# Block 1's scan in chunks of 64 tokens, with the feed-forward down product and the gate product inside it

## The chip, the cores and the metric

The kernel runs on one NeuronCore of one Trainium2 chip. The metric is the device time of one execution in microseconds; the median of the runs shown is taken. TensorE is PE here (PEld its weight loads), VectorE DVE, ScalarE ACT, GpSimd POOL, and SyncE SP, which only issues DMAs.

## The reference, cut to what matters

Block 0 (a top-k attention and a mixture of 64 experts) takes most of the time and is hardly touched. Block 1, on 2 x 512 tokens of 256 channels, is

```
xn = layernorm(x)
r, k, v = mixes of xn and the previous token, times Wr, Wk, Wv    # 32 heads of 8
g = silu(mix @ Wg.T)
w = exp(-exp(time_decay)); u = time_faaaa
step(state, (rc, kc, vc)):                      # one chunk of Q tokens, per head
    att = rc @ kc * w_mat                       # w^(i-j-1) for i > j, u for i == j, else 0
    yc  = att @ vc + rc @ state * w^i
    state = w^Q * state + (kc * w^(Q-1-j)) @ vc
y  = group-normalised over each head of 8 channels, * gamma + beta
x  = x + (y * g) @ Wo.T + relu(xn @ Wfc.T)^2 @ Wproj.T             # ternary Wfc, Wproj
```

The chunk length Q doesn't change the values, apart from rounding.

## The kernel before, in words

Each engine has its own program, and semaphores tie them together; nothing is reordered by a planner. After the last expert, SP loads the routed sums back (racc), then the five weights of block 1 (w5), the decay, bonus and mix rows (s_l1c) and gamma and beta. DVE adds the sums, takes statistics and applies the layer norm (L880), POOL raises the variance to -0.5 (rsqrt, L529), PE transposes and runs the feed-forward up products, and ACT writes relu (L793) and, between them, the decay masks wmask, one exp of 128 columns for each of the 32 heads (L795). DVE squares the relu (L1155) and mixes (mixture, L1170).

Then PE runs, each for all eight token tiles of 128: k and r transposed (project_T), the feed-forward down product, transposes of k (L1548), the v product and the g product (L1312 is the helper product's line for all of these). DVE adds the down product to xs (L1198), scales k (kn, L1211), and adds the bonus to the diagonal of each head's mask (L1216); ACT copies v and takes tanh of g, and DVE multiplies (L1221). All banks are shared in turn.

The scan has 16 units u: token tile t = u // 2 and half of the heads f = u % 2. PE writes a unit's scores for 16 heads as four matmuls, one for each group of 32 rows (L1576); DVE multiplies each bank of 512 columns by the mask (L1290); PE adds the state's part (L1586) and the masked scores times v in 32-column tiles (L1592), and the next state's product (L1604), which DVE masks and adds to the decayed state (state_update, L1227, L1228). PE turns y back (y_natural, L1612). The group norm of earlier tiles is spread between the masks: means and variances on DVE (L1243 to L1256), centring on POOL (centred, L608), the square on ACT (L822), the root on ACT (group_std, L818) with a reciprocal and a Newton step on DVE (group_scale, L1263 to L1273), and four products and sums on POOL (gated, L618 to L624). At the end PE transposes z and multiplies by Wo, DVE adds (L1306), and SP stores each tile.

At the very start POOL issues two DMAs that fill the routed tables with zeros (L522), and then runs block 0's two rsqrt (L529).

## Time and profile before

| | us |
|---|---|
| median of 3 runs (603.67 to 606.5) | 604.94 |
| profiled execution, its own time | 603.5 |
| profiled execution, span of the instructions | 601.8 |
| mean granted share of TensorE's clock | 0.892 |

Over the span PE is busy for 457.6 us (76%), DVE for 340.9 (57%), POOL for 344.0 (57%) and ACT for 194.5 (32%). Times of rows are microseconds from the start of the span. A row of a group gives its count (x), what ended the idle time before it (<-), and its mean in ns where it says so. Ends of matmuls are modelled, so the starts are read.

### The profile page before, as it was taken

To read this page: it belongs to the slowest core of one execution; us is meant where nothing else is said; L and a number is where in the kernel's file an instruction comes from. 1 tells how busy PE (TensorE), PEld (TensorE's weight loads), DVE (VectorE), ACT (ScalarE), POOL (GpSimd) and SP (SyncE) were. 2 spreads that over 40 slices of the span, in tenths; PEclk is the share of its full clock that TensorE was granted. 3 is DMA by queue.
4 is the path that set the end of the run, shared out by engine and by line. 5 is a ranking of instruction groups with operands and counts; after the bars stand their busy time and mean duration, and the time that the engine had idled before them with its cause. 6 is when DMAs were issued, how large, how long until landed. Compare 5 with 4: busy or idle time off the path is not lost.

```text
span 601.8 us, 8652 instructions
## 1 busy us (share of the span) xinstructions
PE 457.6 (76%) x2288; PEld 281.7 (47%) x2288; DVE 340.9 (57%) x931; ACT 194.5 (32%) x512; POOL 344.0 (57%) x327
## 2 busy tenths in 40 slices
PE   2840870688878887677678777989489989999977
PEld 1620430255545554444445444658334678455546
DVE  4799995144434444354343543542567548696983
ACT  1423220233424344343343343431074604021112
POOL 6057777777777777777787777752024001033443
PEclk9985795697879989999998997989789999797997
DMA  8511618266878778888787887863500000000002
GB/s 305 213 26 32 169 23 209 58 159 164 210 181 228 193 189 201 206 185 203 179 216 189 193 199 178 223 129 88 186 0 2 0 0 1 1 2 1 2 2 70
DMA packets 49984, 75.40 MB, mean 125 GB/s; under 512 B 14553, under 2 KB 31289, under 8 KB 49785
## 3 DMA queue, kind: packets, MB, share of 16 engines
q1 hardware_dynamic: 32968, 53.74, 30.1%
q0 software_dynamic: 16992, 21.38, 19.2%
q8 instruction: 11, 0.18, 0.1%
q14 instruction: 13, 0.10, 0.1%
HBM read 58.31 MB, written 15.99 MB: 123 GB/s over the span
## 4 chain that ended last, share of the span: by engine, by line
POOL 42%; PE 23%; issue 20%; DVE 8%; DMA 3%; ACT 3%; SPq 0%; POOLq 0%; DVEq 0%; ACTq 0%
POOL big L544 20%; PE ps L1312 14%; POOL routed L558 11%; POOL big L551 10%; PE ps L1576 4%; DVE big L1290 2%; DMA routed<-big 2%; PE ps L1592 2%; DMA big<-in_maa 1%; PE ps L1317 1%; ACT big L795 1%; DVE big L915 1%; DVE big L912 1%; DVE big L919 1%; PE ps L1586 1%
## 5 line engine op out<-in xcount | busy, mean ns | idle before, releaser
L1312 PE MATMUL ps<-big 128*128 128x352 f32 (+4 forms) x768 | 227.8, 445 | 17.7 <-ACT big L719 14.8
L1312 PEld LDWEIGHTS ps<-big 128*128 128x128 f32 (+2 forms) x768 | 147.6, 202 | 78.0 <-ACT big L719 25.4
L544 POOL DMA_INDIRECT big<-val_tab,big x128 | 125.4, 980 | 62.4 <-issue 38.7
L558 POOL DMA_INDIRECT routed<-big x64 | 104.3, 1630 | 34.1 <-issue 17.1
L1020 DVE SCALAR_TENSOR_TENSOR big<-big,ps 128x176 f32<-128x176 f32 x64 | 21.6, 337 | 104.3 <-ACT big L714 104.3
L1317 PE MATMUL ps<-cst,big 128*128 128x128 f32 x144 | 31.4, 307 | 57.7 <-DMA big<-tok_tab,big 55.6
L551 POOL DMA_INDIRECT big<-tok_tab,big x64 | 61.5, 962 | 22.6 <-issue 17.7
L1028 DVE COPY big<-ps 88x256 f32<-88x256 f32 x64 | 26.9, 420 | 67.9 <-PE ps L1404 67.3
L709 ACT ACTIVATE big<-ps 128x256 f32<-128x256 f32 x64 | 24.6, 384 | 110.5 <-PE ps L1317 108.9
L1317 PEld LDWEIGHTS ps<-cst,big 128*128 128x128 f32 x144 | 17.6, 150 | 76.9 <-DMA big<-tok_tab,big 51.9
L1312 PE MATMUL ps<-xnT,big 128*128 128x512 f32 (+1 forms) x104 | 51.4, 652 | 2.1 <-ACT xnT L646 2.1
L719 ACT ACTIVATE big<-ps,big 128x256 f32<-128x256 f32 x64 | 30.2, 472 | 57.6 <-DMA routed<-big 48.9
L1290 DVE TENSOR_TENSOR big<-ps,big 128x512 f32<-128x512 f32 x64 | 42.0, 678 | 2.5 <-PE ps L1576 2.2
L1576 PE MATMUL ps<-big 32*128 32x512 f32 x128 | 36.3, 697 | 3.0 <-DVE big L1290 2.0
L725 ACT ACTIVATE big<-ps 128x512 f32<-128x512 f32 x64 | 34.5, 595 | 0.9 <-PE ps L1421 0.8
L714 ACT ACTIVATE big<-ps 128x176 f32<-128x176 f32 x64 | 20.4, 318 | 43.8 <-PE ps L1312 43.4
L1312 PEld LDWEIGHTS ps<-xnT,big 128*128 128x128 f32 (+1 forms) x104 | 20.8, 206 | 28.5 <-issue 26.9
L1404 PE MATMUL ps<-cst,big 128*88 128x128 f32 x128 | 27.0, 295 | 0.0
L1317 PE MATMUL ps<-cst,xn 128*128 128x128 f32 x48 | 10.5, 344 | 20.9 <-DVE xn L880 17.9
L608 POOL TENSOR_TENSOR xn<-xn,gst 128x256 f32<-128x256 f32 x8 | 5.0, 629 | 35.6 <-DVE gst L1246 35.6
L1404 PEld LDWEIGHTS ps<-cst,big 128*88 128x88 f32 x128 | 15.1, 130 | 20.7 <-issue 16.3
L597 POOL MEMSET big<- 128x2560 f32 x1 | 2.2, 2237 | 39.2 <-ACT big L809 39.2
(179 smaller groups left out, 617.2 us busy)
## 6 DMA issues: line engine op xcount, KB each, us to landing
big<-in_w SPq DMA_DIRECT2D x64, 352.0 KB
big<-in_w SPq DMA_DIRECT2D x64, 160.0 KB
big<-q_dram SPq DMA_DIRECT2D x144, 32.0 KB
routed<-big POOLq DMA_DIRECT2D x2, 1152.0 KB, 12.3
big<-val_tab,big POOLq DMA_INDIRECT x128, 2.3
big<-routed SPq DMA_DIRECT2D x4, 512.0 KB, 4.6
q_dram<-big SPq DMA_DIRECT2D x24, 64.0 KB
tok_tab<-xn SPq DMA_DIRECT2D x1, 1280.0 KB, 5.5
```

Of the source, the lines that this page charges most:

```text
L544: nc.gpsimd.indirect_dma_start(vals[:, group, side, c, :], None, val_tab, bass.IndirectOffsetOnAxis(ap=vidxT[:, col:col + 1], axis=0))\
L551: nc.gpsimd.indirect_dma_start(xe[:, e % SLOTS, :], None, tok_tab, bass.IndirectOffsetOnAxis(ap=sidx[:, e:e + 1], axis=0))\
L558: nc.gpsimd.indirect_dma_start(routed[e % 2], bass.IndirectOffsetOnAxis(ap=sidx[:, e:e + 1], axis=0), ye[:, e % 2, :], None, compute_op=AL ...
L709: nc.scalar.activation(xeT[:, u % 2, :, :], PS[0][:, 0:D].rearrange("p (c n) -> p c n", c=DC), ACT.Copy).then_inc(s_xeT, 1)
L719: nc.scalar.activation(ye[:, u % 2, :], PS[3][:, 0:D], ACT.Copy, scale=gate).then_inc(s_y, 1)
L725: nc.scalar.activation(ex[:, c, :], PS[4 + c % 2][:, :], ACT.Exp).then_inc(s_ex, 1)
L1028: nc.vector.tensor_copy(heT[:, u % 2, :, :], PS[2][0:IC, 0:2 * P].rearrange("p (c n) -> p c n", c=2))\
L1290: nc.vector.tensor_tensor(aring[:, a % 8, :].rearrange("p (h n) -> p h n", h=4), PS[q][:, :].rearrange("p (h n) -> p h n", h=4), wmask[:, ...
L1312: last = nc.tensor.matmul(o, w, m, start=(n == 0), stop=(n == len(pairs) - 1))
L1317: last = nc.tensor.transpose(bank[:, c * P:(c + 1) * P], src[:, c * P:(c + 1) * P], ident)
L1404: last = nc.tensor.transpose(PS[2][0:IC, c * P:(c + 1) * P], hm[:, u % 2, c * IC:(c + 1) * IC], ident)
L1576: nc.tensor.matmul(PS[q][:, :], kT[rows, f, tok(t)], rhead[rows, f, :, tok(t)], start=True, stop=True).then_inc(s_a1p, 1)
```

## The change

- A chunk is 64 tokens. The two chunks of a token tile lie on partitions 0 to 63 and 64 to 127: scores go as 32 x 64 tiles of 256 columns, outputs as 64 x 32 tiles of 64 columns into two banks, and one mask product covers two banks (masked), so there are two for a unit. wmask is 32 heads of 64 columns.
- The state is kept in a ring of four. PE multiplies the old one by a diagonal matrix of the chunk's decay (wdiag) and adds the new product in the same bank; DVE masks and copies it (state_copy). There are 14 such steps, seven for each batch.
- The feed-forward down product and the g product of each tile are issued in the scan, into PS[7], which y_natural uses as well. ACT copies the down product out (ff_copy), and POOL adds it to xs (x2_add).
- The squares and the causal mask go to POOL, the bonus goes onto the diagonal in eight operations of 512 columns, mixture(3) writes xnT.
- The group norm's root is one pow on POOL (group_rsqrt).
- SP issues the small rows of block 1 ahead of the routed sums; POOL runs block 0's rsqrt ahead of the zero fills.

The core of the diff, with the indent cut; removed functions are shown above:

```diff
 "vrow": H0 * np.array([[S - 1, 0, S + S - 1, S]]) + p,
 "slot": p,
-"jdec": P - 1 - p,
+"jdec": Q1 - 1 - p % Q1,
...
 oT_at = [(), (0, 1, 2), (3, 4, 5), (6, 7)]
 SLOTS = 4
 UNITS = B * TPB * 2
+STATE_AT = []
+for u in range(UNITS):
+    b, n = u // 8, u % 8 + 1
+    STATE_AT.append(7 * b + n if n < NQ - 1 else 7 if u == 7 else None)
...
     for u in range(SLOTS):
         next_weights(E // SLOTS - 1, u, slice(E // SLOTS - 1, E // SLOTS))
     sp.wait_ge(s_lp, NG * 4)
+    sp.wait_ge(s_y, E + 1)
+    sp.dma_start(edrow, td_row.partition_broadcast(P)).then_inc(s_l1c, 16)
+    sp.dma_start(urow, u_row.partition_broadcast(P)).then_inc(s_l1c, 16)
+    sp.dma_start(edcol, td_col).then_inc(s_l1c, 16)
+    sp.dma_start(maat, maa).then_inc(s_l1c, 16)
     for i in range(2):
         sp.wait_ge(s_sc[i], 16 * (1 + E // 2))
         for b in range(B):
             sp.dma_start(racc[i][:, b * TPB:(b + 1) * TPB, :],
                          routed[i][b * S:(b + 1) * S, :].rearrange("(t p) d -> p t d", p=P))\
               .then_inc(s_racc[i][b], 16)
-    sp.wait_ge(s_y, E + 1)
     sp.dma_start(w5, w_rkvgo).then_inc(s_w5, 16)
-    sp.dma_start(edrow, td_row.partition_broadcast(P)).then_inc(s_l1c, 16)
...
     sp.dma_start(gb[:, 0, :], gamma.partition_broadcast(P)).then_inc(s_gb, 16)
     sp.dma_start(gb[:, 1, :], beta.partition_broadcast(P)).then_inc(s_gb, 16)
...
     last.then_inc(s_fill, 1)
     pool.wait_ge(s_fill, 5)
+    def rsqrt(n, half):
+        t = slice(half * TPB, (half + 1) * TPB)
+        pool.wait_ge(s_var, B * n + half + 1)
+        nc.gpsimd.tensor_tensor(rstd[:, 1, t], rstd[:, 0, t], rsm[:, 2, t], ALU.pow).then_inc(s_rstd, 1)
+    for half in range(B):
+        rsqrt(0, half)
     for i in range(2):
         nc.gpsimd.dma_start(routed[i].rearrange("(r p) d -> p r d", p=P),
                             zero[:, 0:D].rearrange("p (a d) -> p a d", a=1).broadcast_to([P, PAD // P, D]))\
           .then_inc(s_sc[i], 16)
...
     last.then_inc(s_wh, 1)
-    pool.wait_ge(s_wm1, 1)
...
+    def square(i):
+        pool.wait_ge(s_relu, i + 1)
+        h = hf[:, i % FC, (i // FC) * S:(i // FC + 1) * S]
+        nc.gpsimd.tensor_tensor(h, h, h, ALU.mult).then_inc(s_sq, 1)
+    def causal(i):
+        w = wmask[:, i * HH:(i + 1) * HH, :]
+        pool.wait_ge(s_wm1[i], 1)
+        nc.gpsimd.tensor_tensor(w, w, const("causal").unsqueeze(1).broadcast_to([P, HH, Q1]), ALU.mult)\
+          .then_inc(s_wmc, 1)
+    for i in range(4):
+        square(i)
+    causal(0)
+    square(4)
+    causal(1)
+    for i in range(FC, 2 * FC):
+        square(i)
+    nc.gpsimd.memset(gst[:, 2, 0:H1], -0.5)
+    nc.gpsimd.memset(vpr[0], 0.0).then_inc(s_vd, 1)
     pool.wait_ge(s_mix, 4)
+    nc.gpsimd.memset(vpr[1], 0.0).then_inc(s_vd, 1)
     pool.wait_ge(s_v1, NT)
-    nc.gpsimd.memset(vpr, 0.0).then_inc(s_vd, 1)
-    pool.wait_ge(s_vd, 1)
+    pool.wait_ge(s_vd, 2)
     def heads_and(t, k):
...
+    def group_rsqrt(t):
+        pool.wait_ge(s_gv, t + 1)
+        g = [gst[:, k, (t % 4) * H1:(t % 4 + 1) * H1] for k in range(2)]
+        nc.gpsimd.tensor_tensor(g[1], g[0], gst[:, 2, 0:H1], ALU.pow).then_inc(s_gr, 1)
     def gated(t):
         z = xn[:, t, 0:D]
         y, g = heads_and(t, 1)
+        group_rsqrt(t)
         if t == 0:
             pool.wait_ge(s_gbh, 1)
...
+        pool.wait_ge(s_g, t + 1)
         pool.wait_ge(s_gr, t + 1)
         nc.gpsimd.tensor_tensor(y, y, g, ALU.mult).then_inc(s_zs, 1)
...
+            x2_add(t - 1)
         if t >= 2:
             centred(t - 2)
         if t >= 3:
             gated(t - 3)
+    x2_add(NT - 1)
     centred(NT - 2)
     gated(NT - 3)
...
+    def ff_copy(t):
+        act.wait_ge(s_ffd, t + 1)
+        if t >= 2:
+            act.wait_ge(s_x2, t - 1)
+        nc.scalar.activation(ffo[:, t % 2, :], PS[7][:, 0:D], ACT.Copy).then_inc(s_ffo, 1)
+    def gate_tanh(t):
         act.wait_ge(s_gp, t + 1)
...
+        nc.scalar.activation(gn[:, t, :], PS[7][:, 0:D], ACT.Tanh, scale=0.5).then_inc(s_gt, 1)
...
+    def y_copy(t):
+        act.wait_ge(s_ynp, t + 1)
+        nc.scalar.activation(xn[:, t, 0:D], PS[7][:, 0:D], ACT.Copy).then_inc(s_yn, 1)
     for t in range(NT):
         for f in range(2):
             u = 2 * t + f
-            act.wait_ge(s_yTp, u + 1)
...
+            (ff_copy, gate_tanh)[f](t)
+            act.wait_ge(s_yTp, 2 * u + 2)
+            nc.scalar.activation(yTs[:, u % 4, :, :], ps[:, 4:6, 0:Q1], ACT.Copy).then_inc(s_yT, 1)
             if t >= 1:
-                (group_squares, group_std)[f](t - 1)
...
+                (y_copy, group_squares)[f](t - 1)
+    y_copy(NT - 1)
     group_squares(NT - 1)
     for t in range(NT):
-        if t == 2:
-            group_std(NT - 1)
         act.wait_ge(s_zTp, t + 1)
...
     ln_apply(1, 1)
-    def square(i):
...
+    def diagonal(i):
+        dve.wait_ge(s_wmc, i // 2 + 1)
+        h = slice(8 * i, 8 * i + 8)
+        link(nc.vector.tensor_tensor(udiag, const("diag").unsqueeze(1).broadcast_to([P, 8, Q1]),
+                                     urow[:, h].unsqueeze(2).broadcast_to([P, 8, Q1]), ALU.mult))
+        link(nc.vector.tensor_tensor(wmask[:, h, :], wmask[:, h, :], udiag, ALU.add))
     for i in range(4):
         f, n = divmod(i, 2)
         dve.wait_ge(s_kTp, i + 1)
         nc.vector.tensor_copy(kT[:, f, n * S:(n + 1) * S], PS[i][:, :]).then_inc(s_kf, 1)
-    mixture(2)
     for i in range(4):
...
         dve.wait_ge(s_rTp, i + 1)
-        nc.vector.tensor_tensor(rw[:, f, cols].rearrange("p (t n) -> p t n", n=P),
...
+        nc.vector.tensor_tensor(rw[:, f, cols].rearrange("p (t n) -> p t n", n=Q1),
+                                PS[4 + i][:, :].rearrange("p (t n) -> p t n", n=Q1),
+                                wb[:, f, :].unsqueeze(1).broadcast_to([P, NQ, Q1]), ALU.mult).then_inc(s_rw, 1)
...
-    mixture(3)
...
                                 kdec.unsqueeze(2).broadcast_to([P, H1, HN]), ALU.mult).then_inc(s_kn, 1)
-    dve.wait_ge(s_wmc, 1)
...
+    for i in range(4):
+        diagonal(i)
+    dve.wait_ge(s_wall, 1)
+    for f in range(2):
+        note(nc.vector.tensor_scalar(wdiag[:, f, :], ident, wall[:, f:f + 1], None, ALU.mult))
     settle()
-    for t in range(NT):
+    mixture(3)
+    def gate(t):
         dve.wait_ge(s_gt, t + 1)
-        nc.vector.scalar_tensor_tensor(gn[:, t, :], gn[:, t, :], 1.0, PS[t % 4][:, 0:D], ALU.add, ALU.mult)\
+        nc.vector.scalar_tensor_tensor(gn[:, t, :], gn[:, t, :], 1.0, PS[7][:, 0:D], ALU.add, ALU.mult)\
           .then_inc(s_g, 1)
-    def state_update(u):
...
+    def state_copy(k):
+        b, n = divmod(k, NQ - 1)
+        dve.wait_ge(s_kvp, k + 1)
+        nc.vector.tensor_tensor(state[:, (NQ * b + n + 1) % 4, :, :],
+                                PS[6][:, 0:2 * P].rearrange("p (f n) -> p f n", f=2),
+                                const("heads").unsqueeze(1).broadcast_to([P, 2, P]), ALU.mult)\
+          .then_inc(s_st, 1)
     def norm_parts(t):
...
+    norm_stages = (group_means, group_variances)
+    def masked(u, k):
+        a = 2 * u + k
+        dve.wait_ge(s_a1p, 4 * a + 4)
+        if a >= 8:
+            dve.wait_ge(s_yTp, 2 * (a // 2 - 3))
+        h = HH * (u % 2) + 8 * k
+        nc.vector.tensor_tensor(aring[:, a % 8, :].rearrange("p (q n) -> p q n", q=2),
+                                ps[:, 2 * k:2 * k + 2, 0:4 * Q1],
+                                wmask[:, h:h + 8, :].rearrange("p (q h) n -> p q (h n)", q=2),
+                                ALU.mult).then_inc(s_a1, 1)
+    state_copy(0)
     for u in range(UNITS):
-        if u % 8 == 0:
...
         for q in range(4):
-            a = 4 * u + q
...
+            if q % 2 == 0:
+                masked(u, q // 2)
+            elif q == 1:
+                if STATE_AT[u - 1:u] and STATE_AT[u - 1] is not None:
+                    state_copy(STATE_AT[u - 1])
+                if u >= 2 and u % 2 == 0:
+                    gate(u // 2 - 1)
             for stage, norm in enumerate(norm_stages):
                 t, odd = divmod(u - 3 - stage, 2)
                 if t >= 0 and not odd:
                     norm(t, q)
-        if u >= 1 and (u - 1) % 8 < 6:
...
+    gate(NT - 1)
+    for norm, t in ((group_variances, NT - 2), (group_means, NT - 1), (group_variances, NT - 1)):
         for step in range(4):
             norm(t, step)
     for t in range(NT):
         dve.wait_ge(s_op, t + 1)
+        dve.wait_ge(s_x2, t + 1)
         nc.vector.tensor_tensor(xs[:, t, :], PS[4 + t % 4][:, 0:D], xs[:, t, :], ALU.add).then_inc(s_o, 1)
...
-        product(PS[t % 4][:, 0:D], [(hf[:, c, tok(t)], w_pj1[:, c, :]) for c in range(FC)]).then_inc(s_ffd, 1)
...
         if t >= 4:
             pe.wait_ge(s_kn, t - 3)
         for f in range(2):
-            last = nc.tensor.transpose(PS[4 + t % 4][:, f * P:(f + 1) * P], kT[:, f, tok(t)], ident)
+            last = nc.tensor.transpose(PS[t % 4][:, f * P:(f + 1) * P], kT[:, f, tok(t)], ident)
         last.then_inc(s_knp, 1)
...
...
+        product(PS[t % 4][:, 0:D], [(mixed(2, c, tok(t)), w5[:, 2, c, :]) for c in range(DC)])\
+            .then_inc(s_v1p, 1)
+    def ff_down(t):
+        pe.wait_ge(s_sq, FC * (1 + t // TPB))
+        if t >= 1:
...
+            pe.wait_ge(s_g, t)
+        product(PS[7][:, 0:D], [(hf[:, c, tok(t)], w_pj1[:, c, :]) for c in range(FC)]).then_inc(s_ffd, 1)
+    def gate_product(t):
+        pe.wait_ge(s_mix, 4)
+        pe.wait_ge(s_yn, t) if t else pe.wait_ge(s_ffo, 1)
+        product(PS[7][:, 0:D], [(mixed(3, c, tok(t)), w5[:, 3, c, :]) for c in range(DC)]).then_inc(s_gp, 1)
+    def chunk(t, c):
+        return slice(t * P + c * Q1, t * P + (c + 1) * Q1)
+    def scores(u, k):
         t, f = divmod(u, 2)
-        for q in range(4):
...
+        if u:
+            pe.wait_ge(s_a1, 2 * (u - 1) + k + 1)
+        for q in (2 * k, 2 * k + 1):
             rows = slice(RG * q, RG * (q + 1))
-            nc.tensor.matmul(PS[q][:, :], kT[rows, f, tok(t)], rhead[rows, f, :, tok(t)],
-                             start=True, stop=True).then_inc(s_a1p, 1)
+            for c in range(2):
+                nc.tensor.matmul(PS[q][c * Q1:(c + 1) * Q1, 0:4 * Q1], kT[rows, f, chunk(t, c)],
+                                 rhead[rows, f, :, chunk(t, c)], start=True, stop=True).then_inc(s_a1p, 1)
     def outputs(u):
         t, f = divmod(u, 2)
         b, g = divmod(t, TPB)
-        y = PS[4 + u % 2]
...
+        if u >= 1:
+            pe.wait_ge(s_yT, u)
+        for c in range(2):
+            n = 2 * g + c
+            if n:
+                pe.wait_ge(s_st, 7 * b + n)
+                nc.tensor.matmul(PS[4 + c][:, 0:Q1], state[:, (NQ * b + n) % 4, f, :], rw[:, f, chunk(t, c)],
+                                 start=True, stop=False, skip_group_check=True)
+        pe.wait_ge(s_a1, 2 * u + 2)
+        pe.wait_ge(s_vd, t + 3)
         for h in range(4):
-            for q in range(4):
...
+            for c in range(2):
+                rows = slice(c * Q1, (c + 1) * Q1)
+                for q in range(4):
+                    at = (q % 2 * 4 + h) * Q1
+                    last = nc.tensor.matmul(PS[4 + c][32 * q:32 * q + 32, 0:Q1],
+                                            vpr[t % 2][rows, 4 * f + q, 32 * h:32 * h + 32],
+                                            aring[rows, (2 * u + q // 2) % 8, at:at + Q1],
+                                            start=(h == 0 and 2 * g + c == 0), stop=(h == 3),
+                                            skip_group_check=True)
+                if h == 3:
+                    last.then_inc(s_yTp, 1)
+    def state_product(k):
+        b, n = divmod(k, NQ - 1)
+        t, c = divmod(NQ * b + n, 2)
+        rows = slice(c * Q1, (c + 1) * Q1)
+        if k:
+            pe.wait_ge(s_st, k)
+        if n:
+            for f in range(2):
+                nc.tensor.matmul(PS[6][:, f * P:(f + 1) * P], wdiag[:, f, :], state[:, (NQ * b + n) % 4, f, :],
+                                 start=(f == 0), stop=False, skip_group_check=True)
+        for f in range(2):
+            last = nc.tensor.matmul(PS[6][:, f * P:(f + 1) * P], kn[rows, t, f * P:(f + 1) * P],
+                                    vn[rows, t, f * P:(f + 1) * P], start=(n == 0 and f == 0), stop=True,
+                                    skip_group_check=True)
+        last.then_inc(s_kvp, 1)
     def y_natural(t):
         pe.wait_ge(s_yT, 2 * t + 2)
-        if t >= 1:
-            pe.wait_ge(s_yn, t)
+        if t < NT - 1:
+            pe.wait_ge(s_ffo, t + 2)
+        else:
+            pe.wait_ge(s_g, NT)
         for f in range(2):
-            last = nc.tensor.transpose(PS[7][:, f * P:(f + 1) * P], yTs[:, f, 0:P], ident)
+            last = nc.tensor.transpose(PS[7][:, f * P:(f + 1) * P],
+                                       yTs[:, (2 * t + f) % 4, :, :].rearrange("p c n -> p (c n)"), ident)
         last.then_inc(s_ynp, 1)
-    pe.wait_ge(s_g, NT)
     pe.wait_ge(s_v1, NT)
-    scores(0)
+    pe.wait_ge(s_rh, 4)
+    scores(0, 0)
+    scores(0, 1)
+    state_product(0)
     for u in range(UNITS):
         if u + 1 < UNITS:
-            scores(u + 1)
+            scores(u + 1, 0)
+        (ff_down, gate_product)[u % 2](u // 2)
+        if u + 1 < UNITS:
+            scores(u + 1, 1)
+        outputs(u)
+        if STATE_AT[u] is not None:
+            state_product(STATE_AT[u])
         if u >= 2 and u % 2 == 0:
             y_natural(u // 2 - 1)
-        outputs(u)
-        state_product(u)
     y_natural(NT - 1)
     def z_transposes(t):
         pe.wait_ge(s_z, t + 1)
         if t == 0:
-            pe.wait_ge(s_a1, 4 * UNITS)
+            pe.wait_ge(s_a1, 2 * UNITS)
         if t >= 2:
             pe.wait_ge(s_zT, t - 1)
         transposes(xn[:, t, 0:D], PS[t % 2], s_zTp)
```

## Rows read from the trace of the kernel before

**Rows 1.** the page, its first line.

```profile
span 601.8 us, 8652 instructions
```

**Rows 2.** busy time by stage, busy us (x) of each engine.

```profile
...
474.90:492.20 17.30, 17.30 (x83) 15.18 (x82) 4.02 (x10) 6.21 (x11) 0.00 (x0) 1.00 0.00 0
511.70:582.70 71.00, 67.58 (x710) 37.41 (x710) 59.60 (x147) 12.22 (x36) 20.99 (x34) 0.90 0.01 2
582.70:601.80 19.10, 12.19 (x50) 9.67 (x50) 8.90 (x24) 4.30 (x14) 8.59 (x13) 0.82 0.16 55
```

**Rows 3.** the chain of waits by line, 566 to 575 us.

```profile
...
by line: DVE big L1290 48.6%; issue 20.8%; DVE gst L1253 9.0%; DVE gst L1256 7.8%; DVE big L1227 4.7%; DVE gst L1243 3.7%; DVE gst L1263 2.9%; DVE gst L1266 1.2%; DVE gst L1273 1.1%; DVE gst L1246 1.0%; DVE big L1228 0.7%; DVEq L1288 0.7%; 
```

**Rows 4.** groups by line on DVE in the scan.

```profile
...
L1290 DVE TENSOR_TENSOR big<-ps,big 128x512 f32<-128x512 f32 x64 | 42.0, 678 | 2.5 <-PE ps L1576 2.2 <-issue 0.2
```

**Rows 5.** PE in one unit; x4: to 522.99, x12: to 523.2.

```profile
...
522.44 0.49 PE L1586 MATMUL ps<-big 128*128 128x128 f32 x2
...
522.86 0.32 PE L1592 MATMUL ps<-big 128*32 128x128 f32 x4
...
522.86 0.54 PE L1592 MATMUL ps<-big 128*32 128x128 f32 x12
...
522.86 1.08 PE L1592 MATMUL ps<-big 128*32 128x128 f32 x32
523.87 0.49 PE L1604 MATMUL ps<-big 128*128 128x128 f32 x2
```

**Rows 6.** the chain of waits before the scan: start, us, what.

```profile
...
496.88 13.99 PE ps L1312 x64
...
513.01 0.70 DVE big L1290
```

**Rows 7.** DVE in order of time before the scan: start, us, line.

```profile
...
474.92 0.69 DVE L1193 TENSOR_TENSOR big<-ps,wb 128x512 f32<-128x512 f32 x1 [1.02 <-PE ps L1312]
...
492.52 2.47 DVE L1170 SCALAR_TENSOR_TENSOR big<-big,xnT 128x1024 f32<-128x1024 f32 x2
494.91 2.74 DVE L1211 TENSOR_TENSOR big<-ps,big 128x256 f32<-128x256 f32 x8
```

**Rows 8.** DVE and POOL side by side in the scan.

```profile
...
566.86 0.73 POOL L622 TENSOR_TENSOR xn<-xn,gb 128x256 f32<-128x256 f32 x1
566.92 0.70 DVE L1256 TENSOR_SCALAR gst<-gst 128x32 f32<-128x32 f32 x1
```

**Rows 9.** after the last expert, in order of time.

```profile
...
414.33 9.78 SPq L491 DMA_DIRECT2D big<-routed  x4
...
418.57 0.47 ACT L719 ACTIVATE big<-ps,big 128x256 f32<-128x256 f32 x1 [7.83 <-PE ps L1312]
...
430.75 1.05 POOL L529 TENSOR_TENSOR rstd<-rstd,rsm 128x4 f32<-128x4 f32 x1 [9.87 <-DVE rstd L875]
433.76 0.23 ACT L779 ACTIVATE big<-big 128x32 f32<-128x32 f32 x1 [14.72 <-DMA big<-in_maa]
...
434.67 1.37 DVE L880 TENSOR_SCALAR xn<-xs,mv,rstd 128x256 f32<-128x256 f32 x4
```

**Rows 10.** the start of the kernel, in order of time.

```profile
...
5.84 2.34 POOL L522 DMA_DIRECT2D routed<-big  x2 [0.32 <-POOL big L517]
...
8.32 2.18 POOL L529 TENSOR_TENSOR rstd<-rstd,rsm 128x4 f32<-128x4 f32 x2
```

**Rows 11.** busy time of PE during the 64-column products.

```profile
...
28.25:31.60 3.35, 3.35 (x32) 1.00 0.45 160
```

**Rows 12.** groups of weight loads, two stretches.

```profile
...
L1312 PEld LDWEIGHTS ps<-big,xnT 128*128 128x128 f32 x55 | 8.1, 191 | 0.6
...
L1592 PEld LDWEIGHTS ps<-big 128*32 128x32 f32 x512 | 14.2, 117 | 3.6 <-DVE big L1290 1.4 <-issue 0.5
```

**Rows 13.** ACT's last square, in order of time.

```profile
...
587.11 0.42 ACT L822 ACTIVATE big<-xn 128x256 f32<-128x256 f32 x1 [2.81 <-POOL xn L608]
```

**Rows 14.** groups on POOL: busy us, mean ns.

```profile
...
L529 POOL TENSOR_TENSOR rstd<-rstd,rsm 128x4 f32<-128x4 f32 x4 | 4.2, 1060 | 17.5 <-DVE rstd L875 17.4
```

More of the change, by code:

```diff
@@ L57 @@
 CONST = {}
-for _name, _n in (("ident", P), ("pdist", P), ("steps", P), ("heads", P), ("tokinv", NT), ("vrow", 4), ("slot", 1),
+for _name, _n in (("ident", P), ("pdist", 64), ("steps", 64), ("diag", 64), ("causal", 64), ("heads", P), ("tokinv", NT), ("vrow", 4), ("slot", 1),
                   ("jdec", 1), ("hrow", NV4)):
@@ L336, in block_kernel @@
         s_kdec = sem("key_decay_exp")
-        s_wm1 = sem("decay_tables_exp")
+        s_wall = sem("chunk_decay_exp")
+        s_wm1 = [sem(f"decay_tables_exp{i}") for i in range(2)]
         s_wmc = sem("decay_mask_causal")
```

183 lines of the change are left out of this document (42 added, 141 removed).

## The prediction

> **What bounds the kernel now.** I read the span first [rows 1], then busy time by stage [rows 2], because the change touches only the part after the experts (from 424 us on) and one line at the start. Four stages follow each other there: the feed-forward down products (474.9 to 492.2), a short step of transposes, the v and g products (to 511.7), the scan (to 582.7) and a tail. In the first PE is busy throughout at full clock: it is worth what PE takes. The third is so too, as the next part shows. The scan is different. Its chain of waits is nearly half mask multiplications on DVE, L1290, and the rest is small DVE work [rows 3]; these multiplications, 64 of 0.68 us, idle only 2.5 us ahead of them [rows 4]. PE also reads 67.6 of 71 us there, but most of that is scores that stand behind a mask still to be freed. So the scan is DVE's, at 71 / 16 = 4.4 us a unit (a token tile and half of the heads), and PE's own need must be added up.
>
> **What PE needs per unit.** One unit's PE rows [rows 5]: the 32 output instructions (each matmul is two passes) start in fours (from 522.86 on, four by 522.99 and twelve by 523.20): one four each 0.11. Eight fours are 0.87 us, and the next product starts 1.01 us after the first: a block of small tiles costs 0.14 over its passes. A state product, two passes of 0.107 on the full array between tiled blocks, takes 0.42: a full block costs 0.2 over its passes, its first weight load being uncovered. PE now needs scores 0.99 + state 0.42 + outputs 1.01 + state product 0.42 + 0.14 = 3.0 us of 4.4.
>
> **The change, ahead of the scan.** The down products leave (17.3 us [rows 2]) and the eight g products (32 instructions at 13.99 / 64 = 0.219 us, 7.0 us [rows 6]); they come back below. What then ends this stretch is DVE. It finishes r's multiplication at 475.6 [rows 7], then mixture(2) 2.5 (478.1), gamma and beta 0.4, eight kn 2.7 (481.3). diagonal() issues eight 128x512 operations, each followed by its own wait: priced like L1290 with 0.07 for the wait, 6.0 (487.3). wdiag 0.4, mixture(3) 2.5 (490.2), first state copy and first mask 1.2: 491.4. PE has the v products at 487.3 and the first scores at 488.3, and waits. Today the first mask ends at 513.7 [rows 6]. That is 22.3 us less, whatever stands in the loop. The squares and the causal mask go to POOL: ten 128x512 products at some 1.3 us and two of 1024 columns at 2.5 us, scaled from 0.73 us for 256 [rows 8], 18 us between 442 and 466; they are needed in the loop only (s_sq) and by diagonal (480), so they cost nothing; uncovered, the last of them could be 14 us later before anything waits.
>
> **Two moved queues.** SP issues the four block 1 rows ahead of the loads of routed. Today the last of them lands at 433.7, and behind it stand ACT's exp and then, on DVE, three small operations ahead of ln_apply(1,0), which starts at 434.67 though rstd was there at 431.8 [rows 9]. The gain is at most 2.9. But routed's first two loads, now issued at 414.3, come behind the last expert's scaled output (419.0) and four issues of 0.5 us, at about 421; with 4.6 us to land, DVE's three routed additions start 2.5 us late, and end about 1 us late, since the last waited for its own load before. I take 1.6; bounds 0 and 2.9. At the start POOL's two rsqrt pass the zero fills (5.84 to 8.2 [rows 10]): DVE can go on at 8.4 instead of 9.4, when it has done the second half's statistics: 1.0, handed on through the top-k, bounds 0 and 1.9. Together 2.6.
>
> **The loop after.** Per unit, at full clock:
> - scores: twice four matmuls of 256 columns, two passes of 0.216, + 0.14: 1.14
> - down product (even units) 17.3 / 8 = 2.16 + 0.2; g product (odd) 0.87 + 0.2
> - state part of the outputs: four instructions of 64 columns on full weights. The nearest row says that these don't get shorter with the columns: 3.35 us for about 31 of them, 0.11 each [rows 11]: 0.45 + 0.2 = 0.65
> - outputs: 64 instructions of 64 columns in 32-column tiles on half the rows. If eight run side by side, eight groups of 0.054 to 0.11; a 32-column load takes 0.12 against 0.19 for 128 columns [rows 12], so it isn't what held the row above at 0.11. I take 0.06: 0.48 + 0.14 = 0.62. Upper bound: the halves take turns, 16 groups at 0.11, 1.9
> - state product: four passes on the decay's full weights, four on half the rows, each 0.43 + 0.2: 1.26
> - y_natural (even) 0.27.
>
> A pair is 6.30 + 4.74 = 11.04, eight pairs 88.3; the last unit has no scores (1.14), three loop units no state product and one no decay (4.4), four units only one state read (0.9), and unit 0 no y_natural (0.3): 81.6. Waits: an even unit's down product stands behind gate() on DVE, which is queued behind state_copy: 0.3 to leave PE, 0.35, 0.42, hand-overs 0.06, against 0.77 for the switch and scores: 0.35 x 7 = 2.4. Some 0.1 at each of 14 state steps: 1.4. The granted clock was 0.90 over the scan's 71 us [rows 2]: with levels of 1.2 and 2.4 GHz that is 14 us at the low one, or 7 lost, around PE's waits at its start and for the second batch's first mask. The new loop has one such start, and full products in it: I take 2.5; bounds 0 and 10. Sum 87.9, against 69.0 from the first mask today. DVE needs two masks 1.36, state copy 0.45, half a gate 0.2 and half the means and variances 0.6: 2.6 us a unit of 5.5, so it is no bound.
>
> The scan ends 22.3 + 2.6 - 18.9 = 6.0 us earlier.
>
> **The tail and pow.** Today ACT's last square ends at 587.53 [rows 13] and the kernel 14.3 us later, 19.1 after the last outputs. group_scale's ACT and DVE steps become one pow on POOL, on 32 columns. The trace has pow on 4: 1.06 us [rows 14], where an addition of 256 takes 0.73 [rows 8]. Lower bound 1.06 (all fixed), upper 8 x 0.95 + 0.1 = 7.7 (all by column). The nearest row is pow's own, so I take 2.0, twice that. A gated() is then 3.15 + p long. After the last outputs (T) POOL has centred(6), gated(5), centred(7) at T + 2.6 + p, gated(6), gated(7): z of the last tile at T + 9.55 + 3p, end at T + 13.9 + 3p; the other way, over the last square, it ends at T + 18 + p. With p = 2: T + 20.0 by either, 0.9 more than today. In the loop POOL needs 5 + p a tile of 11: covered up to p = 5.5.
>
> **A rule against the change.** A DVE tensor_scalar on 32 columns took 0.70 and ended with POOL's addition beside it [rows 8]. The Trainium skill (SBUF — State Buffer, Who interferes with whom) says that the pair is an exclusive lock held for a whole instruction, taken by fast DVE modes and by DVE operations with two SBUF inputs; this trace agrees for the first. By it, mixtures would stand behind squares on POOL; at 451 to 457 POOL waits for exps anyway, and the masks read PSUM, so it adds nothing to the sum except that means and variances can wait for a pow, with 5 us of slack a pair.
>
> **Sum.** 601.8 - 6.0 + 0.9 = 596.7 us span; the profiled execution took 603.5, 1.7 over its span, and the median is 1.4 above that: 599.8 us.
>
> **Rivals.**
> - pow by column (0.18). For: 4 columns of pow already cost more than 256 of an addition. Against: the fixed part may be most of it. From p = 3.7 the end at T + 13.9 + 3p has eaten the whole gain; at 7.7 it is T + 37, 17 more than forecast, and POOL bounds the loop too: 616 to 620. This decides the other side: slower. The Trainium skill (GPSIMD Engine Reference, Performance pitfalls for Q7 kernels) says that a dependent fp32 chain pays about 4 cycles for each element, which speaks for this case; no row here shows pow on more than 4 columns.
> - The output tiles don't run eight at a time (0.10). For: no row has tiles on half the rows. 1.9 instead of 0.62 adds 20: 620; two turns of short groups (16 x 0.06) add 0.48 x 16 = 7.7: 607.
> - The clock stays low in more of the loop, as small tiles follow each other, or PE's waits for ACT and DVE around the one bank PS[7] are longer than 0.35 (0.14): 5 to 8 us more, 605 to 608.
> - The forecast, 0.58: 590 to 606.
>
> The low end has pow at 1.1 (-0.9), no lost clock and no waits (-6.3), outputs at 0.054 (-0.8) and more from the moved queues (-1.8): 590. The high end reaches into the first two rivals, 614.
>
> Within 0.5% (3.0 us) is what a measurement of this kernel can't tell from no change: 601.9 to 608.0. Faster is most of the forecast's case, 0.53; same its upper end, two turns of tiles and the third rival, 0.19; slower pow and turns of full length, 0.28.
>
> **What would show it.** Loop pairs near 11 us, the down product 0.35 behind a gate; output starts in eights; DVE under two thirds busy in the scan, against 84% now; pow's mean near 2; the first mask's end near 489, the last outputs near 577; ACT's last exp no longer waiting for block 1's rows. I am wrong first if pow is long or the outputs come in fours.

## The result, and the profile after

The changed kernel took 613.12 us (median of 4 runs, 611.8 to 614.01), the kernel before 605.72 beside it: a ratio of 1.0113, 95% interval 1.0057 to 1.0169. A second comparison gave 1.018 (1.0145 to 1.0216). It is slower by 7 to 11 us; 599.8 was forecast, with slower at 0.28. Ratios below are to the kernel before on the same chip. That kernel's own runs spread over 597 to 610 us, and the first outputs of the scan began anywhere from 492 to 498 us in versions of the changed kernel that are the same up to there. So the experiments are also read by two stretches inside one execution: from the start of the first outputs to the start of the last (83.6 us in the changed kernel, in each of four profiles: twice as it is, e2 and e5), and from the end of the last outputs, T, to the end of the span. I call the second one the tail.

The span of the profiled execution (own time 611.8 us) stands against [rows 1]; the two windows, columns as in [rows 2], hold the loop and the tail.

```profile
span 610.0 us, 10034 instructions
...
487.90:577.50 89.60, 86.29 (x1523) 60.08 (x1526) 33.52 (x78) 14.84 (x44) 54.70 (x50) 0.98 0.01 2
577.50:610.00 32.50, 14.25 (x88) 10.45 (x80) 5.31 (x15) 4.24 (x12) 24.58 (x16) 0.68 0.10 33
```

The scan is now PE's (96% busy, DVE 37%), and the last outputs start at 577.08 and last 0.86 (the line below): T = 577.9, 4.7 us earlier than the 582.7 before. The tail is 32.1 us against 19.1, 13.0 more. 13.0 - 4.7 = 8.3, and the spans differ by 8.2. So the whole loss is in the tail, and there POOL is busy for 24.6 of 32.5 us.

```profile
577.08 0.86 PE L1625 MATMUL ps<-big 64*32 64x64 f32 x64
```

The two tails repeat from profile to profile: 19.0 to 19.1 us in three profiles where the tail is as before, 32.1 in both of the changed kernel. T doesn't: where nothing but the tail or idle POOL time was touched in the kernel before, it was at 577.2 (e1) and 577.5 (e10) as well. So the 4.7 us of this pair of profiles are no measure of what the change gains up to T; the ratios give one at the end of the experiments.

POOL's groups, from the scan to the end (busy us, mean ns, idle before):

```profile
L647 POOL TENSOR_TENSOR gst<-gst 128x32 f32<-128x32 f32 x8 | 43.5, 5442 | 0.0
L660 POOL TENSOR_TENSOR xn<-xn,gb 128x256 f32<-128x256 f32 x8 | 5.8, 727 | 0.6
```

L647 is pow on 32 columns: 5.44 us, against 1.06 on 4 columns in [rows 14] and the 2.0 that the forecast took. A product of 256 columns takes 0.73. The chain of waits in the tail shows three of them one behind the other, for tiles 5, 6 and 7 (start, us, what):

```profile
576.26 0.63 POOL xn L642
576.89 5.41 POOL gst L647
...
582.43 0.64 POOL xn L658
...
585.47 0.59 POOL xn L642
586.05 5.41 POOL gst L647
...
594.64 5.41 POOL gst L647
...
603.27 0.69 PE ps L1350 x2
603.96 3.43 PE ps L1345 x8
```

Inside the scan, the same view over a pair of units. The reader is to see that every piece but one short stretch is PE's: scores (L1604), state part (L1616), outputs (L1625), state product (L1642 the decay, L1645 the new part), y_natural (L1657), with down (x10) and g (x4) under L1345.

```profile
546.08 0.42 DVE big L1264
...
546.63 2.40 PE ps L1345 x10
549.03 0.59 PE ps L1604 x8
549.62 0.59 PE ps L1616 x4
550.21 0.79 PE ps L1625 x53
551.00 0.64 PE ps L1642 x4
551.64 0.64 PE ps L1645 x4
552.28 0.37 PE ps L1657 x2
...
553.24 1.08 PE ps L1345 x4
...
558.50 1.53 PE ps L1345 x6
```

From one down product to the next is 558.50 - 546.63 = 11.87 us. What PE still waits for in the scan, in us, times and longest, is DVE's gate, L1264:

```profile
PE ps L1345 <- DVE big L1264: 2.7, 7, 0.7
```

After the last expert, ACT's exp follows the four small loads and the layer norm starts 3.2 us earlier than the 434.67 of [rows 9]:

```profile
416.82 1.55 POOL L574 DMA_INDIRECT routed<-big  x1 [7.30 <-ACT big L766]
...
422.58 0.23 ACT L826 ACTIVATE big<-big 128x32 f32<-128x32 f32 x1 [6.04 <-DMA big<-in_maa]
423.93 1.23 DVE L1173 TENSOR_TENSOR xs<-xs,big 128x1024 f32<-128x1024 f32 x1 [3.12 <-DMA big<-routed]
...
431.45 1.38 DVE L929 TENSOR_SCALAR xn<-xs,mv,rstd 128x256 f32<-128x256 f32 x4
```

But POOL's scatter of the last expert (the first line) is 2.5 us earlier too. Before, it was

```profile
419.32 1.55 POOL L558 DMA_INDIRECT routed<-big  x1 [7.30 <-ACT big L719]
```

From the scatter to the layer norm it is 14.6 us, and 15.35 before (14.95 in e1 and in e10, which have the order of before).

### The profile page after: what moved, and what is told of

It reads as the page before. It is cut to its first block, busy times and chain, and to the rows that moved or that the text cites. A ratio compares the mean times of both kernels' runs of the same rounds, so it can differ in the third digit from the quotient of the medians.

```text
span 610.0 us, 10034 instructions
## 1 busy us (share of the span) xinstructions
PE 463.8 (76%) x3032; PEld 288.9 (47%) x3032; DVE 300.0 (49%) x807; ACT 193.0 (32%) x511; POOL 400.8 (66%) x356
## 3 DMA queue, kind: packets, MB, share of 16 engines
q0 software_dynamic: 16992, 21.38, 19.1%
## 4 chain that ended last, share of the span: by engine, by line
POOL 41%; PE 25%; issue 20%; DMA 6%; DVE 6%; ACT 2%; POOLq 0%; ACTq 0%; DVEq 0%
POOL big L560 19%; PE ps L1345 15%; POOL big L567 9%; POOL routed L574 9%; DMA routed<-big 4%; POOL gst L647 3%; PE ps L1604 2%; PE ps L1625 2%; PE ps L1645 1%; PE ps L1616 1%; PE ps L1642 1%; PE ps L1350 1%; DVE big L964 1%; DVE big L961 1%; DMA big<-routed 1%
## 5 line engine op out<-in xcount | busy, mean ns | idle before, releaser
L1345 PE MATMUL ps<-big 128*128 128x352 f32 (+3 forms) x736 | 227.0, 454 | 18.5 <-ACT big L766 13.6
L1345 PEld LDWEIGHTS ps<-big 128*128 128x128 f32 (+1 forms) x736 | 143.5, 206 | 82.3 <-issue 27.0
L756 ACT ACTIVATE big<-ps 128x256 f32<-128x256 f32 x64 | 24.6, 385 | 97.8 <-PE ps L1350 97.3
L1345 PE MATMUL ps<-xnT,big 128*128 128x512 f32 (+1 forms) x104 | 52.2, 660 | 2.1 <-ACT xnT L693 2.1
L647 POOL TENSOR_TENSOR gst<-gst 128x32 f32<-128x32 f32 x8 | 43.5, 5442 | 0.0
L1345 PE MATMUL ps<-big,xnT 128*128 128x256 f32 (+1 forms) x128 | 32.3, 401 | 8.2 <-ACT xnT L889 7.6
L1345 PEld LDWEIGHTS ps<-xnT,big 128*128 128x128 f32 (+1 forms) x104 | 20.9, 207 | 28.6 <-issue 27.0
L1345 PEld LDWEIGHTS ps<-big,xnT 128*128 128x128 f32 x128 | 23.9, 216 | 15.1 <-ACT xnT L889 7.9
L1437 PEld LDWEIGHTS ps<-cst,big 128*88 128x88 f32 x128 | 15.4, 132 | 22.3 <-issue 18.0
L1312 DVE TENSOR_TENSOR big<-ps,big 128x512 f32<-128x512 f32 x32 | 21.1, 683 | 4.2 <-PE ps L1604 4.2
```

The costliest lines, as they stand in the source:

```text
L647: nc.gpsimd.tensor_tensor(g[1], g[0], gst[:, 2, 0:H1], ALU.pow).then_inc(s_gr, 1)
L756: nc.scalar.activation(xeT[:, u % 2, :, :], PS[0][:, 0:D].rearrange("p (c n) -> p c n", c=DC), ACT.Copy).then_inc(s_xeT, 1)
L1345: last = nc.tensor.matmul(o, w, m, start=(n == 0), stop=(n == len(pairs) - 1))
L1437: last = nc.tensor.transpose(PS[2][0:IC, c * P:(c + 1) * P], hm[:, u % 2, c * IC:(c + 1) * IC], ident)
```

## The experiments

The leading theory (A) is that pow on 32 columns, three times in POOL's queue behind the last outputs, is the loss. Its rivals: pow is only slow beside other work (B in the first), the tail is long for other reasons (B in the second), the scan itself is the loss (C).

**What pow costs by its size.** The kernel before, with seven unused pows on POOL before the scan:

```diff
+nc.gpsimd.memset(gst[:, 0, 0:64], 0.7)
+nc.gpsimd.memset(gst[:, 1, 0:64], -0.5).then_inc(s_probe, 1)
+for i, n in enumerate((1, 2, 4, 8, 16, 32, 64)):
+    pool.wait_ge(s_probe, i + 1)
+    nc.gpsimd.tensor_tensor(gst[:, 2, 0:n], gst[:, 0, 0:n], gst[:, 1, 0:n], ALU.pow).then_inc(s_probe, 1)
```

> The kernel before, with seven pow instructions of 1, 2, 4, 8, 16, 32 and 64 columns added on POOL while it idles before the scan; the result is not used. Theory A (pow is paid by the column): a line through the two sizes seen so far, 1.07 us at 4 columns and 5.44 at 32, gives 0.6, 0.8, 1.1, 1.7, 2.9, 5.4 and 10.4 us. Theory B (pow itself is short, about 2 us at 32 columns as forecast, and the 5.44 us come from the work beside it in the scan, on the shared SBUF or on a late operand): alone it takes near 2 us at 32 columns and under 3 at 64.

Groups by shape on POOL in that kernel:

```profile
L600 POOL TENSOR_TENSOR gst<-gst 128x64 f32<-128x64 f32 x1 | 10.5, 10547 | 0.1
...
L600 POOL TENSOR_TENSOR gst<-gst 128x32 f32<-128x32 f32 x1 | 5.4, 5426 | 0.1
L600 POOL TENSOR_TENSOR gst<-gst 128x16 f32<-128x16 f32 x1 | 2.9, 2903 | 0.1
...
L600 POOL TENSOR_TENSOR gst<-gst 128x8 f32<-128x8 f32 x1 | 1.6, 1635 | 0.1
...
L600 POOL TENSOR_TENSOR gst<-gst 128x4 f32<-128x4 f32 x1 | 1.0, 1006 | 0.1
...
L600 POOL TENSOR_TENSOR gst<-gst 128x1 f32<-128x1 f32 x1 | 0.6, 570 | 0.1
```

Theory A, on its numbers. From 32 columns to 64 it is 5.12 us more, 0.160 a column; from 16 to 32 it is 0.158; what is left over is 0.3 to 0.4. The 5.43 us come ahead of the scan, where DVE has only a few operations beside it, and with one fixed value (0.7); in the scan it is 5.44. So neither the scan's work nor the values have a part in them.

**Pow on 4 columns in the changed kernel**, and **pow twice**:

```diff
-nc.gpsimd.tensor_tensor(g[1], g[0], gst[:, 2, 0:H1], ALU.pow).then_inc(s_gr, 1)
+nc.gpsimd.tensor_tensor(g[1][:, 0:4], g[0][:, 0:4], gst[:, 2, 0:4], ALU.pow).then_inc(s_gr, 1)
```

> The changed kernel with pow on 4 of the 32 columns, so the other 28 heads are not normalised rightly; all else is issued as before. Theory A (three pows of 5.44 us stand in POOL's queue behind the last outputs): by the forecast's own formula the end comes at T + 18 + p with p = 1.1, 19.1 us behind the last outputs instead of 32.1: 13 us less than the changed kernel, so about 600 us or 0.99 of the kernel before. Theory B (the tail is long for the rest of POOL's queue, its added additions to xs, and for PE at its low clock): at most the last pow leaves the path, 4.4 us less, 608 to 609 us. Theory C (the scan itself is the loss): no change worth the name, 611 to 613.

Measured: 0.993 (0.9897 to 0.9963), 599.35 us, on a chip where the kernel before took 602.95. Scan 83.6 us, unchanged; tail 579.4 to 596.6, 17.3 us instead of 32.1. That is 14.8 us off the tail for 13 expected, and this kernel, in which 28 of the 32 heads miss their root, is faster than the one before: theories B and C fall. The tail beats the 19.1 that was worked out by 1.8. From the last square's end (583.49) it is 13.1 us, where the kernel before took 14.3 with the clock granted at 0.82 in its tail; here it was 0.90:

```profile
579.35:596.60 17.25, 11.05 (x50) 8.85 (x50) 5.59 (x14) 4.22 (x12) 10.95 (x15) 0.90 0.19 62
```

```diff
 nc.gpsimd.tensor_tensor(g[1], g[0], gst[:, 2, 0:H1], ALU.pow).then_inc(s_gr, 1)
+pool.wait_ge(s_gr, 2 * t + 1)
+nc.gpsimd.tensor_tensor(g[1], g[0], gst[:, 2, 0:H1], ALU.pow).then_inc(s_gr, 1)
...
-pool.wait_ge(s_gr, t + 1)
+pool.wait_ge(s_gr, 2 * t + 2)
```

> The changed kernel with each tile's pow issued twice, the same result written twice. Theory A: three more pows of 5.44 us and a wait each behind the last outputs, 16.5 us, and POOL's need for a tile rises to about 12.3 us against 11.9 for a pair of units, which adds up to 3 us more by the end of the scan: 629 to 634 us. Theories B and C: 5.5 us more at most, 618 or less.

Measured: 1.0773 (1.0728 to 1.0819), 650.28 us. The direction is A's, the size a miss. The tail is 53.3 us, 21.2 more; the scan is 100.9 us from first to last outputs, 17.3 more, where up to 3 were expected. My need of POOL for a tile was wrong: from the groups of the changed kernel it is 5.44 + 0.63 (centring) + 2.81 (the four products) + 0.73 (x2_add) + 0.40 (copy of v) = 10.0, with some 0.5 of hand-overs 10.5, not 6.8. A second pow makes it 15.9; centrings follow each other at 567.61 and 583.47, 15.86 apart, and PE waits (clock 0.86 in the loop's window, from 0.98). So with one pow POOL is covered in the scan by only 1.4 us a pair (11.87 - 10.5).

**The two queue moves alone**, in the kernel before:

```diff
+for half in range(B):
+    rsqrt(0, half)
 for i in range(2):
     nc.gpsimd.dma_start(routed[i]...)
-for half in range(B):
-    rsqrt(0, half)
...
 sp.wait_ge(s_lp, NG * 4)
+sp.wait_ge(s_y, E + 1)
+sp.dma_start(edrow, ...)   # and urow, edcol, maat
 for i in range(2):
     sp.wait_ge(s_sc[i], 16 * (1 + E // 2))
```

> The kernel before with the two queue moves alone (the four small loads of block 1 ahead of the loads of the routed sums, and POOL's two early root operations ahead of the zero fills). The forecast's term: 2.6 us less, so 603.1; from the changed kernel's trace, where the layer norm of block 1 starts 3.2 us earlier, 3.2 less. Rival: what comes first is given back where PE waits for the value projections and the feed-forward products anyway, 0 to 0.5 us.

Measured: 0.9962 (0.9923 to 1.0001), 600.67 us: 2.3 us less, near the forecast's 2.6, though the interval just reaches no change. The rival's 0 to 0.5 isn't excluded by it. The traces show the two moves apart. Behind the top-k PE starts at 61.9, 61.9 and 62.9 us in the three profiles with POOL's old order, and at 60.4 to 62.1 in the eleven with the new one, 1.2 earlier on average, for 1.0 forecast. From the last scatter to the layer norm it is 15.35, 14.95 and 14.95 with SP's old order and 14.5 to 14.9 with the new one, 0.4 less on average, where 1.6 was taken.

**The roots of the last three tiles off POOL.** Tiles 0 to 4 keep pow; behind the last tanh ACT takes three roots, and DVE does the reciprocal and the Newton step (group_scale as before):

```diff
-group_rsqrt(t)
+if t < NT - 3:
+    group_rsqrt(t)
...
 y_copy(NT - 1)
+group_std(NT - 3)
+group_std(NT - 2)
 group_squares(NT - 1)
+group_std(NT - 1)
```

> The changed kernel with the roots of the last three tiles as in the kernel before (ACT takes the root, DVE the reciprocal and a Newton step), behind the last tanh; tiles 0 to 4 keep pow. Theory A (three pows of 5.44 us on POOL behind the last outputs are the loss): POOL has only the products left, three tiles of 3.15 us and a centring, the last of them done about 13 us behind the last outputs, the end about 18 behind them instead of 32: 14 us less than the changed kernel, 0.988 of the kernel before or about 598 us. Theory C (the scan is the loss): 1 to 4 us less, not under 1.005.

Measured: 1.0038 (1.0005 to 1.0071), 603.18 us. Better than the changed kernel, but two thirds of what was expected: the tail is 576.5 to 599.0, 22.5 us, which is 9.6 less than 32.1 and not 14. Its chain of waits tells why:

```profile
577.31 0.38 ACT xn L882
577.71 1.28 ACT L878
579.01 0.24 ACT gst L878
...
584.42 0.43 ACT big L872
...
586.07 0.28 ACT xnT L899
...
586.39 2.07 PE ps L1373 x4
588.47 0.43 PE ps L1378 x2
...
594.65 1.74 PE ps L1373 x8
```

Two things that I hadn't counted. ACT loads a function table when it goes from tanh to the root (1.28 us, ahead of the first root; the second line of the chain). And the end is no longer POOL's: the eight output products go one behind the other on PE from ACT's first copy of transposed z, and that copy (L899) stands in ACT's queue behind the last tile's square (L872) and root, though z of tiles 0 and 1 had been transposed at 577.7. The kernel before has the same order: its last square, then the copy at 587.44.

**gate() ahead of state_copy** in DVE's queue, in the changed kernel:

```diff
-if STATE_AT[u - 1:u] and STATE_AT[u - 1] is not None:
-    state_copy(STATE_AT[u - 1])
 if u >= 2 and u % 2 == 0:
     gate(u // 2 - 1)
+if STATE_AT[u - 1:u] and STATE_AT[u - 1] is not None:
+    state_copy(STATE_AT[u - 1])
```

> The changed kernel with gate() ahead of state_copy in DVE's queue in the even units; pow is untouched. By the forecast's term the down product waits 0.35 us for a gate seven times (2.4 us); the gate comes 0.45 earlier so, which takes all of it: 2 us less than the changed kernel, a ratio of about 1.008. Rival: state_copy is late by 0.42 instead, the next state reads wait for it, and nothing is gained (1.011).

Measured: 1.0137 (1.0095 to 1.0178), which can't tell 2 us from none. The profile can: from the first outputs to the last it is 80.97 us instead of 83.61, 2.6 less, and PE's down products wait 0.3 us for the gate in all, where it was 2.7 (group of the changed kernel, then of this one):

```profile
L1345 PE MATMUL ps<-big 128*128 128x256 f32 x80 | 20.9, 412 | 2.7 <-DVE big L1264 2.7
```

```profile
L1345 PE MATMUL ps<-big 128*128 128x256 f32 x80 | 19.4, 389 | 0.3 <-DVE big L1264 0.3
```

**All eight roots on ACT**, in the scan too:

```diff
-                group_rsqrt(t)
...
                         (y_copy, group_squares)[f](t - 1)
+                    if f == 0 and t >= 2:
+                        group_std(t - 2)
...
-norm_stages = (group_means, group_variances)
+norm_stages = (group_means, group_variances, group_scale)
```

> The changed kernel with all eight roots on ACT and DVE as in the kernel before, so that ACT goes from tanh to the root and back for each tile in the scan. Theory A: the tail as with the last three alone, 18 us, and a ratio of 0.985 to 0.99 if going back and forth costs ACT nothing. If it costs ACT something, ACT's copies of the bank PS[7] are late and the scan is longer: then the ratio lies above that of the last three alone, and the scan's window shows longer than 89.6 us.

Measured: 1.0392 (1.0321 to 1.0463), 622.4 us. The tail is short (18.9 us), and the scan 104.2 us, 20.6 longer. ACT now loads a table before each root and again before each tanh. Groups on ACT in the scan, and what PE waits for there:

```profile
L870 ACT ACT_TABLE_LOAD x5 | 6.4, 1283 | 0.1
L860 ACT ACT_TABLE_LOAD x5 | 6.4, 1283 | 0.1
```

```profile
PE ps L1626 <- DVE big L1333: 9.5, 5, 1.9
```

```profile
492.36:597.60 105.24, 92.36 (x1519) 63.81 (x1518) 37.68 (x106) 31.18 (x61) 25.41 (x41) 0.88 0.01 2
```

The way is: table load, late root, and in DVE's queue the mask (L1333) behind the reciprocal that waits for it; PE then waits for a mask at each of the five tiles, and its clock, granted at 1.00 from the first outputs on in the changed kernel, is at 0.88 in that window. These waits are 9.5 us, and PE's busy time is 92.4 us, 11.2 more than in the changed kernel; together they are about the 20.6. The Trainium skill (ScalarE: Activation LUTs, What ACT_TABLE_LOAD costs) gives 1283 ns for a load, which the trace repeats, and 1.38 us for a drain beside it, which the trace doesn't show: in the chain above the copy is over at 577.69, the load begins at 577.71 and the root at 579.01.

**A version meant to beat both.** Last three roots on ACT, gate first, and the last tile's centring and products on DVE, so that POOL has two tiles to finish (e8):

```diff
 centred(NT - 2)
 gated(NT - 3)
-centred(NT - 1)
 gated(NT - 2)
-gated(NT - 1)
...
+nc.vector.tensor_tensor(zh, zh, gl, ALU.subtract).then_inc(s_gc, 1)
...
+link(nc.vector.tensor_tensor(zh, zh, gl, ALU.mult))
+link(nc.vector.tensor_tensor(z, z, gb[:, 0, :], ALU.mult))
+link(nc.vector.tensor_tensor(z, z, gb[:, 1, :], ALU.add))
+nc.vector.tensor_tensor(z, z, gn[:, NT - 1, :], ALU.mult).then_inc(s_z7, 1)
```

Then, since PE's row of output products was what ended last, ACT's first two z copies ahead of its last square, together with the last tile's variance ahead of the scale of tile 6 and one output addition ahead of DVE's products (e9), and the z copies alone in the kernel before (e10, and e12 with the queue moves):

```diff
 group_std(NT - 3)
 group_std(NT - 2)
-group_squares(NT - 1)
-group_std(NT - 1)
 for t in range(NT):
+    if t == 2:
+        group_squares(NT - 1)
+        group_std(NT - 1)
     act.wait_ge(s_zTp, t + 1)
```

> Roots of the last three tiles on ACT and DVE, gate() first, and the last tile's centring and four products on DVE, which is idle behind the last outputs, so that POOL has two tiles to finish there. The two chains side by side end about 9.5 us behind the last outputs, the kernel about 14.5 behind them; with the scan 2 us shorter: 576 + 14.5 + 1.7 outside the span = 592 us, 0.977 of the kernel before. If DVE's products and POOL's slow each other down on the shared port, up to 3 us more.

> The kernel of the best so far, with ACT's copies of the first two transposed z tiles ahead of the last square in its queue (they are ready 5 us before), the last tile's variance ahead of the sixth tile's scale on DVE, and the first output addition ahead of the last tile's products. Theory: what ended last there was no longer POOL but the eight output products on PE, which follow each other at 1.08 us from ACT's first copy on, and that copy stood behind the last square. With it 4 to 5 us earlier the last z tile sets the end: about 16.5 us behind the last outputs instead of 20.8, a ratio of about 0.988. Rival: the last z tile's chain is as late as PE's, 1 us or less is gained, 0.993.

> The kernel before, with ACT's copies of the first two transposed z tiles ahead of the last square. Theory: its tail is set in the same way; the first output product starts 3.1 us earlier (584.7 instead of 587.85) and the last z tile, ready 3.3 us before its transposes, just doesn't bind: 3 us less, 0.995. Rival: the square and the root behind it come later and hand the time back, 0 (1.000).

> The changed kernel as it is, on the same chip as the two others: 1.011 of the kernel before by the first comparison, with 83.6 us from the first outputs to the last and 32 us behind them. Nothing here depends on a theory.

> The kernel before with only the two queue moves and ACT's first two z copies ahead of the last square; scan, products and roots as they were. If the two add up: 0.9962 x 0.9954 = 0.992, as much as the best version with chunks of 64 (0.9918), and then the chunks themselves are worth nothing that can be measured once the roots are off POOL. If the chunks are worth the 6 us by which the last outputs came earlier, this one stays at 0.992 and a version with both the chunks and as short a tail would be 0.984; the best one's tail of 19.4 us against 16.2 here is then where it stays behind.

| | ratio, 95% interval | first to last outputs | tail |
|---|---|---|---|
| changed kernel again (e11) | 1.0180, 1.0145 to 1.0216 | 83.6 | 32.1 |
| e8: roots, gate, DVE takes the last tile | 0.9946, 0.9918 to 0.9974 | 81.0 | 20.8 |
| e9: and the z copies first | 0.9918, 0.9886 to 0.9950 | 81.0 | 19.4 |
| kernel before (first profile) | 1 | 63.3 | 19.1 |
| e10: before, z copies first | 0.9954, 0.9916 to 0.9992 | 61.5 | 16.2 |
| e12: before, both queue moves, z copies first | 0.9932, 0.9891 to 0.9972 | 62.9 | 16.1 |

e10 is as expected: the tail is 2.9 us shorter for one changed order of ACT's queue (its 61.5 us from first to last outputs owe nothing to that: e1 had 61.5 too, and e4 62.9); the first output product starts at 579.46, 2.0 us behind T, and at 587.85, 5.2 behind, in the kernel before. e12 holds this and the queue moves together, at the sum that was expected within its interval. e8 and e9 beat the kernel before, but by less than expected (0.977 and 0.988): their tails are 20.8 and 19.4 us, for 14.5 and 16.5. In e9 the chain runs over the roots' small steps on DVE, three tiles in a row, and two of PE's products wait for an output addition that stands behind these steps in DVE's queue. The second then runs with PE's clock low, at 2.04 us instead of 1.10:

```profile
588.88 1.10 PE L1391 MATMUL ps<-big,xnT 128*128 128x256 f32 x4 [1.43 <-DVE xs L1375]
...
591.70 2.04 PE L1391 MATMUL ps<-big,xnT 128*128 128x256 f32 x4 [1.19 <-DVE xs L1375]
```

e9 (0.9918) is the fastest run, but can't be told from e12 (0.9932), which has the scan, the chunks and the roots of the kernel before. What the change gains up to T can be worked out from the ratios: the time against the kernel before, less what the tail differs by. It is 6, 2, 2 and 1 us in the changed kernel, e11, e2 and e5 (2.9 on average), 4.5 to 5.2 in the three with gate() first (e6, e8, e9), and 2 and 1 with the queue moves alone (e4, e12). Each of these is uncertain by 2 to 3.5 us. So the chunks, for all the code they move, are worth an estimated 1 us beyond the queue moves, which isn't clear of the noise, and gate() first some 2 more. e2 and e12 side by side say the same: both have the queue moves, e2 the chunks and a tail of 17.3 us, e12 the old scan and 16.1, and they stand at 0.993 both. A version with the chunks, right values and a tail of 16 us wasn't built.

## Why the prediction was wrong

The step that failed is the size of one term: "The nearest row is pow's own, so I take 2.0, twice that." Pow on 32 columns takes 5.44 us, 2.7 times as much. The direction followed from that term alone, and the break-even was in the text (p = 3.7). Put into the forecast's own formula, T + 13.9 + 3p gives 30.2 us; measured 32.1. The other 1.9 is what is left of two misses. The last tile's z was done 24.5 us behind T, where the formula has 25.9, and the rest took 7.6 us, where it has 4.35. More than half of that excess is PE's clock (0.68 over the tail): the last two tiles' products are one row of eight instructions, 3.43 us in the chain above, where the same eight take 1.74 at full clock (the last line of e5's chain). The forecast of 599.8 was 13.3 us too low: 12.1 in the tail (20.0 forecast) and, in this profile, 1.2 at T. By the ratios T came some 3 us earlier instead of 6.0; two terms that fell short, the loop (2.1) and SP's move (1.2), add up to about that. The measured 613.1 lies just under the 614 named as the high end; that end was stretched towards this rival, and it is the forecast's direction that failed.

I had given this case 0.18 and priced it at 616 to 620 for p = 7.7. The rows offered the slope only as a range, 0 to 0.95 us for four columns (0.24 each), since pow stood at a single size. Twice the price of 4 columns was no estimate from rows; it was the choice of a value near the lower end. A value half-way in the range (4.4) would have been past the break-even.

Point by point, the rest:

- The first mask: forecast to end at 488.8, ended at 487.8. From the layer norm to there it is 56.4 us, 79.0 before: 22.7 less, for 22.3 forecast. diagonal(), mixture(3) and the v products took what was said, and DVE did end this stretch. Right. The queue moves are right only in sum and within a wide interval (e4: 2.3 us for 2.6): the 3.2 us at the layer norm are mostly chance between two executions, POOL's move gave 1.2 for 1.0, and SP's gave 0.4 for 1.6.
- The loop: 87.9 us forecast, 90.0 measured (487.9 to 577.9). The pair is 11.87 us for 11.04 + waits. Measured (forecast): scores 1.18 a unit (1.14), down 2.40 (2.36), g 1.08 (1.07), state product 1.28 (1.26), state part 0.59 (0.65), y_natural 0.37 (0.27), outputs 0.79 (0.62). These 0.17 in 16 units are 2.7 us, the only term off by more than 0.1. With 0.79 us, neither the 1.9 of full turns nor the 1.1 of short ones has come, so the rival of 0.10 is out. That eight tiles run side by side isn't shown: the 64 starts of a block are spread over 0.7 us (550.14 to 550.81), some 0.01 us apart, and don't come in eights.
- The gate wait: 0.35 x 7 = 2.4 forecast, 2.7 measured in seven waits, and 2.6 given back when gate() went first (e6). The clock in the loop was granted at 0.98, where the scan before had 0.90, so it cost 1.8 us of 89.6 for the 2.5 taken. The rival of 5 to 8 us more from waits and clock (0.14) is out.
- The lock rule: a DVE tensor_scalar of 32 columns averages 474 ns in the scan before (L1256), beside POOL's additions. After, the same operation (L1301) takes 0.17 to 0.18 us, and five of the six in the scan start and end inside a pow. Means and variances didn't wait for pow, which the prediction's rule of an exclusive lock left open; here the measurement goes against the rule.
- "In the loop POOL needs 5 + p a tile": 10.4 at p = 5.44, measured 10.5, and covered, by 1.4 us a pair; e3 shows that the cover ends there.
- What the forecast didn't see: the tail before the change was bounded by eight output products behind a square in ACT's queue. It was worth 2.9 us (e10), about as much as the queue moves, and it capped what taking pow away could give (e5).

## What to carry to other kernels

An operation that a trace shows at one size has an unknown slope. Before it is moved to a larger size, look whether its price at the small one can be all fixed cost; if the break-even lies inside the range, the sign is open, and a probe of a few sizes settles it at no cost. Put a slow operation where it is covered and out of the last tiles' chain: pow was harmless for five tiles in the scan and cost 13 us for the last three. After a long stage is shortened, read the queue order of each engine in the tail, since one square ahead of a copy that had long been ready cost 3 us in the kernel before.
